# Two context-attention layers: score matmuls as 64 by 64 tiles, keys two batches ahead through a scratch in device memory

## The reference, cut to what matters

```python
# L3_xattn (L1_xattn: no _l2norm, no bq, scores times D**-0.5, a boolean mask instead of attn_bias)
q = (x @ Wq + bq).reshape(B, Lq, H, D).transpose(0, 2, 1, 3)     # B=8, Lq=64, H=16, D=16
k = (y @ Wk).reshape(B, Ly, H, D).transpose(0, 2, 1, 3)          # Ly=1601
v = (y @ Wv).reshape(B, Ly, H, D).transpose(0, 2, 1, 3)
q = _l2norm(q) * scale_mul
k = _l2norm(k)
attn = jnp.einsum('bhqd,bhkd->bhqk', q, k) + attn_bias
attn = jax.nn.softmax(attn, axis=-1)
oup = jnp.einsum('bhqk,bhkd->bhqd', attn, v)
return oup.transpose(0, 2, 1, 3).reshape(B, Lq, C) @ Wo + bo
```

## Time and profile before

| what | value |
|---|---|
| median of 3 runs | 2486.56 us (2485.36 to 2490.42) |
| the profiled execution | 2501.07 us, span 2499.3 us |
| PE busy in the span | 2236.3 us (89%) |
| PEld, DVE, ACT, POOL busy | 57%, 66%, 50%, 32% |
| batches 0 to 7 of the first layer, from the first L3417 of each | 386.05 to 726.26 us |
| the same of the normed layer | 1863.67 to 2258.00 us |

### The profile page before, as it was taken

One profiled execution on the slowest core, in us unless ns is written; L12 is line 12 of the kernel. 1 busy time (PEld: TensorE's weight loads), 2 busy tenths in 40 slices (PEclk: granted clock), 3 DMA queues, 4 the chain that ended last, 5 costly groups with the idle time before them and its releaser, 6 DMA issues. The chain is left out here.

```text
span 2499.3 us, 50978 instructions
## 1 busy us (share of the span) xinstructions
PE 2236.3 (89%) x20593; PEld 1417.7 (57%) x20650; DVE 1650.0 (66%) x3182; ACT 1243.2 (50%) x2071; POOL 808.3 (32%) x660
## 2 busy tenths in 40 slices
PE   6885779999978889999999999699879999998898
PEld 4764445666654555656655666356546555566554
DVE  4987456555548756888888854644576666665577
ACT  2326234555554225555555554566436555563565
POOL 5610052233206112321233300045445455433254
PEclk8998899999989989999999999899999999999999
DMA  3200453423313047676776764133322323220231
GB/s 113 71 7 1 144 136 103 107 78 106 79 66 106 13 118 144 121 133 133 151 146 122 125 113 80 34 102 102 116 67 67 86 69 86 69 67 23 71 96 60
DMA packets 358618, 226.84 MB, mean 91 GB/s; under 512 B 289913, under 2 KB 326610, under 8 KB 358386
## 3 DMA queue, kind: packets, MB, share of 16 engines
q1 hardware_dynamic: 355314, 215.20, 35.5%
q0 software_dynamic: 3072, 8.39, 1.2%
HBM read 114.87 MB, written 0.52 MB: 46 GB/s over the span
## 5 line engine op out<-in xcount | busy, mean ns | idle before, releaser
L3950 POOL TENSOR_TENSOR l2x_rows<-l2x_rows,l2x_one 128x256 f16<-128x256 f32 (+1 forms) x91 | 89.2, 1006 | 379.6 <-DVE l2x_rows L1507 354.5
L100 PE MATMUL PS<-hot 128*128 128x512 f16 x460 | 134.3, 427 | 82.1 <-DVE l0a_g L1119 17.5
L4054 PE MATMUL PS<-l2x_rows,l2x_pth 128*128 128x512 f16 x832 | 200.3, 379 | 1.7 <-DVE l2x_mean L4263 1.7
L3711 DVE CUSTOM_DVE_ANT_0 l1x_junk<-PS,l1x_bias 128x1024 bf16<-128x1024 f32 (+1 forms) x128 | 123.2, 991 | 73.6 <-PE PS L3371 72.7
L4256 DVE TENSOR_TENSOR l2x_pl<-l2x_sc,l2x_ph 128x1664 f16<-128x1664 f32 x64 | 125.1, 1954 | 44.6 <-ACT l2x_ph L4133 43.9
L4151 ACT ACTIVATE l2x_meanT<-PS 128x256 f32<-128x256 f32 x64 | 24.5, 383 | 250.5 <-PE PS L4016 250.5
L4241 DVE CUSTOM_DVE_ANT_0 l2x_sc<-PS,l2x_bias 128x1665 f32<-128x1665 f32 x64 | 120.9, 1889 | 36.3 <-issue 35.0
L3711 DVE CUSTOM_DVE_ANT_0 l3x_junk<-PS,l3x_bias 128x1024 bf16<-128x1024 f32 (+1 forms) x128 | 123.6, 991 | 24.3 <-PE PS L3371 21.6
L4008 PE MATMUL PS<-l2x_kh,l2x_qth 128*128 128x512 f16 (+1 forms) x512 | 131.9, 339 | 1.5 <-issue 1.5
L4008 PE MATMUL PS<-l2x_kh,l2x_qtl 128*128 128x512 f16 (+1 forms) x512 | 131.9, 339 | 0.0
L4008 PE MATMUL PS<-l2x_kl,l2x_qth 128*128 128x512 f16 (+1 forms) x512 | 131.9, 339 | 0.0
(11 more groups left out here) (866 smaller groups left out, 6109.0 us busy)
## 6 DMA issues: line engine op xcount, KB each, us to landing
l2f_unit<-in_L_ffn_units_dram SPq DMA_DIRECT2D x36, 384.0 KB, 3.1
l3f_unit<-in_L_ffn_units_dram SPq DMA_DIRECT2D x34, 384.0 KB, 3.0
l1x_kst<-l1x_kh SPq DMA_DIRECT2D x128, 100.1 KB, 2.2
l3x_kst<-l3x_kh SPq DMA_DIRECT2D x128, 100.1 KB, 2.2
l2x_rows<-in_ctx_dram SPq DMA_DIRECT2D x8, 1536.0 KB
l1x_ctx<-in_ctx_t_dram SPq DMA_DIRECT2D x7, 1601.0 KB, 7.3
l3x_ctx<-in_ctx_t_dram SPq DMA_DIRECT2D x7, 1601.0 KB, 7.0
l1x_kst<-l1x_kl SPq DMA_DIRECT2D x64, 100.1 KB, 2.2
```

The lines of the kernel that those rows point to most:

```text
L100: self.nc.tensor.matmul(self.PS[:, bank, :], self.hot[:, 0:P], self.hot[:], start=True, stop=True)
L3711: v.tensor_tensor_reduce(junk[:, slot(it), 0:n], slot_banks(it)[:, 0:n], bias[:, 0 if normed else b % 2, at:at + n], 1.0, LOWEST, ALU.add, ...
L3950: last = nc.gpsimd.tensor_tensor(high[:, at], of[:, at], one[0:p, at].unsqueeze(2).unsqueeze(3).to_broadcast([p, i, NC, P]), ALU.mult)
L4054: nc.tensor.matmul(PS[:, ACC, :], pth[:, u % 2, m, :], rows2[:, b % 2, :, :, m, :], start=(m == 0), stop=False)
```

## The change

Score matmuls work on one head each: 49 rows (high, low, the maximum's row at 32, high) against 64 columns, with the heads of a pair in rows 0 to 48 and 64 to 112 of `qst` and `kst`, and outputs in partitions 0 to 63 or 64 to 127. `A` becomes 4 pairs of pairs by 4 chunks of 401 keys, four matmuls and two VectorE reductions each. `turned` is one block for both halves, and its next call waits until both were read. Keys are made two batches ahead (K, N, I, U of batch b+2 in batch b, later in `steps`; batch 0 makes those of batches 1 and 2, by `opening_steps` and `second_keys`). `kh` and `kl` are written to a scratch `spill` in device memory and read back in six DMAs per chunk, with one semaphore per chunk. ACT and DVE do both halves' work of tile m first and then the items of both steps. The context is split in two parts of columns. In the normed layer the bias goes in as high and low part by two sets of matmuls. `ON_VECTOR` stays at tiles 0 to 3 in both layers.

```diff
-    A = [("A", u, h) for u in range(R) for h in range(NH)]
+    A = [("A", v, j) for v in range(QV) for j in range(NCH)]
     if normed:
-        steps = [[("K", 0, 0)], [("K", 0, 1)], [("N", 0, 0), R_], [("N", 0, 1), ("I", 0, 0)], [("U", 0, 0), ("I", 0, 1), ("V", 0, 0)],
-                 [E, ("U", 0, 1)], [("V", 1, 0)], [("K", 1, 0)], [("K", 1, 1)],
-                 [O_, ("N", 1, 0)], [("N", 1, 1), ("I", 1, 0)], [("U", 1, 0), ("I", 1, 1), ("V", 2, 0)],
-                 [P_, A[0], ("U", 1, 1)], [A[1], A[2]], [("V", 3, 0)], [A[3], A[4]], [A[5]], [A[6]], [A[7], A[8]],
-                 [A[9]], [("M", 0, 0), A[10]], [A[11]], [A[12]], [A[13], A[14]], [A[15]], [("M", 1, 0)]]
+        steps = [[V_[0]], [], [R_, V_[1]], [], [E], [V_[2]], [V_[3]], [O_], [A[0]], [A[1], A[2]], [A[3]], [A[4]], [P_, A[5]], [A[6], A[7]],
+                 [K_[0]], [K_[1], A[8]], [N_[0], M_[0]], [N_[1], I_[0], A[9]], [U_[0], I_[1], A[10]], [U_[1], K_[2], A[11]],
+                 [K_[3], A[12]], [N_[2], A[13]], [N_[3], I_[2], A[14], A[15]], [U_[2], I_[3]], [U_[3]], [M_[1]]]
+        second_keys = {18: [K_[0]], 19: [K_[1]], 20: [N_[0]], 21: [N_[1], I_[0]], 22: [U_[0], I_[1], K_[2]], 23: [U_[1], K_[3]],
+                       24: [N_[2]], 25: [N_[3], I_[2], U_[2], I_[3], U_[3]]}
...
     else:
-        steps = [[("K", 0, 0)], [], [("K", 0, 1), R_], [("K", 1, 0)], [E], [("K", 1, 1)], [("V", 0, 0)], [O_], [A[0]], [A[1]],
-                 [("V", 1, 0), A[2]], [A[3]], [P_, A[4]], [("V", 2, 0), A[5]], [A[6]], [A[7]], [("V", 3, 0), A[8]], [A[9]],
-                 [("M", 0, 0), A[10]], [A[11]], [A[12]], [A[13]], [A[14]], [A[15]], [], [("M", 1, 0)]]
+        steps = [[V_[0]], [], [R_], [V_[1]], [E], [V_[2]], [V_[3], A[0]], [O_, A[1]], [A[2], A[3]], [A[4]], [A[5]], [A[6]], [P_, A[7]],
+                 [A[8]], [K_[0]], [A[9], M_[0]], [A[10]], [K_[1]], [A[11]], [A[12]], [K_[2]], [A[13]], [A[14]], [A[15], K_[3]], [],
+                 [M_[1]]]
+        second_keys = {20: [K_[0]], 22: [K_[1]], 23: [K_[2]], 25: [K_[3]]}
...
                 def stack(b, c):
+                    sp.wait_ge(spilled[c], (b + 1) * SPILL)
                     if b >= 2:
                         sp.wait_ge(turned_made, (b - 1) * STEPS)
-                    for j in range(RC):
-                        for g, part in enumerate((kh, kl, kh)):
-                            sp.dma_start(kst[g * F:(g + 1) * F, b % 2, c * RC + j, :],
-                                         part[j * F:(j + 1) * F, c, :]).then_inc(stacked[c * RC + j], 16)
+                    for at, x in ((0, 0), (DH, 1), (ROW + 1, 0)):
+                        for r in range(2):
+                            sp.dma_start(kst[r * S + at:r * S + at + DH, b % 2, c * RC:(c + 1) * RC, :],
+                                         spill[x, c].rearrange("(j r d) n -> r d j n", r=2, d=DH)[r]).then_inc(stacked[c], 16)
...
-                        for i, at, n in pieces(*halves[j]):
-                            last = nc.tensor.matmul(PS[:, bank + i, 0:n], qst[0:3 * F, b, c, :, :],
-                                                    kst[0:3 * F, b % 2, c, at:at + n], start=True, stop=True)
+                        at, n = chunks[j]
+                        for i in range(2):
+                            for r in range(2):
+                                rows = slice(r * S, r * S + KROWS)
+                                last = nc.tensor.matmul(PS[i * S:(i + 1) * S, bank + r, 0:n], qst[rows, b, 2 * c + i, :],
+                                                        kst[rows, b % 2, 2 * c + i, at:at + n], start=True, stop=True)
...
+                    for u in range(R):
+                        for at, w_ in keys:
+                            for r in range(2):
+                                rows = slice(r * S, r * S + KROWS)
+                                last = nc.tensor.matmul(PS[at:at + w_, S_BANK + r, u * S:(u + 1) * S],
+                                                        kst[rows, b % 2, u, m * P + at:m * P + at + w_], qst[rows, b, u, :],
+                                                        start=not on_tensor, stop=not on_tensor or u == R - 1, skip_group_check=True)
...
-                            pe.wait_ge(exp_done, e - G2 + 1)
+                            pe.wait_ge(exp_done, e)
...
-                            for it in step_before(b, m * G2 + g):
+                            exp(b, m, g)
+                        for g in range(G2):
+                            for it in at_step(b, m * G2 + g):
                                 item(it)
-                            exp(b, m, g)
```

More of the change, by code:

```diff
@@ L3420, in turned @@
-                    last.then_inc(turned_made, 1)
+                        for x in range(2 if normed else 1):
+                            for at, w_ in keys:
+                                for r in range(2):
+                                    half = slice(r * S, (r + 1) * S)
+                                    of_bias = fsp[half, x, :] if normed else bias[half, b % 2, :]
+                                    nc.tensor.matmul(PS[at:at + w_, S_BANK + r, :], of_bias[:, m * P + at:m * P + at + w_], one_hot[half, :],
+                                                     start=(x == 0), stop=False, skip_group_check=True)
```

264 lines of the change are left out of this document (154 added, 110 removed).

## The result

The changed kernel takes 2805.82 us (2799.44 to 2813.48, four runs) against 2488.49 us of the kernel before on the same chip: ratio 1.1276, 95% interval 1.1242 to 1.131. It is slower by 317 us, where I forecast some 30. Both loops got slower. Windows cut at the first matmul of `turned` (now L3479) of a batch, in the same order as the earlier trace rows: first batch, two middle ones, the last but one and the last; the first layer, then the normed one. Columns: stretch, its length, busy us (instructions) of PE, PEld, DVE, ACT and POOL, granted clock, DMA share, GB/s.

A forecast was written before the change was run, and what follows sets the result against it. PE was taken to bound both loops, with slots and DVE taking over after the change. First layer +0.3 and normed layer +29.7 made +30: 2501.1 to 2531 us profiled, 2516 on the median; range 2463 to 2566.

The forecast's parts named there:

- In the loop they have over a batch's slack: Scratch write and six reads a chunk, some 5 and 8 us, hidden in the loop except the normed layer's first half chunk.
- PE's standing lets the clock fall: Listed as proving the forecast wrong: standing PE drops the clock to its lower level, 1.2 GHz; no size given.
- `turned`: 8 x 56 = 0.45 us a key tile becomes 8 x 32 = 0.26, times 13: PE's `turned` matmuls: sets of four run together at 32 ns instead of 56, saving 2.5 us a batch.
- rival 2: Slower still: only two 64 by 64 tiles run together on PE; 2566, up to 2616 us; chance 0.12.
- the row of `values`: Earlier trace of `values`: four heads in different columns, all rows, 56 ns for four; evidence against only two running together.
- PE's work, less 5.8 and 3.6 us: PE's work a batch falls by 5.8 us in the first layer and 3.6 in the normed one.
- Standing of 10.4 us: PE's summed waits in a first-layer middle batch, behind A, K(0), tiles 9 and 11, the end and small ones.
- rival 1: Faster: PE's standing is half of that walked, excess under 4 us a batch; 2471 us; chance 0.24.
- my walk: Item-by-item schedule of a middle batch: PE work 36.6 plus standing 10.4 us in first layer, 44.5 plus 12.2 in normed.
- Middle batches of 45.7 to 47 and 55.4 to 56.7: Middle-batch lengths, without and with O and P: first layer as before, normed layer 2.3 us longer.
- Batch 0 at 55.5 and 76: First batch of each layer makes two batches' keys: 55.5 us against 42.8, and 76 against 51.7.
- Rival 3: It comes out even: saving 30 us larger than summed, most easily in the normed layer's batch 0; 2487 us; chance 0.11.

The follow-up runs named there:

- e2: Changed kernel, scratch reads from batch 2 on go to 64 partitions of one key unit instead of 16 of four, same bytes, keys misplaced; 2711.01 us, 1.083.
- e3: Changed kernel, scratch laid out so each partition's four units form one contiguous 12.8 KB row, still read into 16 partitions; 2817.85 us, 1.126.
- e4: Kernel before, plus bursts of eight 15- or 16-partition reads in seven first-layer batches, into spare partitions, data unused; 2529.91 against 2504.22 us, 1.0113.
- e15: e2 plus warming matmuls where PE stands: 30 and 37 a middle batch, 5 more ahead of O and 5 ahead of the first key tile; 2693.85 us, 1.0742.
- e18: e15 with the thirteenth key tile's `turned` loop turned round, all 64-key matmuls before the one-key ones; keys misplaced; 2647.81 us, 1.0628.
- e17: e12 with the thirteenth key tile's `turned` loop turned round, all 64-key matmuls before the one-key ones; 2674.71 us, 1.0749.
- e12: Changed kernel's 64 by 64 tiles with the order of the kernel before, no scratch, stacked keys copied on chip by 48 copies a batch; 2707.13 us, 1.0883.
- e14: Kernel before, old tiles, without the products of the weights' low parts in K and V, both layers; 2451.05 against 2503.96 us, 0.9776.

## Why the prediction was wrong

The direction was right and the size was not. On the profiled run I had 2531 us, and it took 2807. The batches account for it: over my figures, the walked batches 1 to 5 lie 87 and 95 us, the first ones 16 and 33, batch 6 16 and 20, batch 7 3 and 2; together 272 of 276. The starts of the loops nearly cancel: the first layer's came 9.6 us sooner (forecast 5), and the stretch between it and the normed layer's grew by 16.7 (forecast 5).

- *"In the loop they have over a batch's slack"* and *"I cost that at nothing; if the cover is gone it is 1 to 3 us a batch."* This is the step that failed most. I took each read by its landing, alone, and asked only who waits for the data. Twelve reads into 16 partitions hold all DMA engines for 19 us at 125 GB/s, and the victim is PE, which needs instructions: 9 to 12 us a walked batch, 111 us in all (changed kernel against e2). e3 excludes the rows, e4 shows that no reader of the data is needed, and the fetches on q8 show what PE waited for. It is 111 of some 290 us; e2, without it, would still have been far outside my range.
- *PE's standing lets the clock fall.* I named it as what would make me wrong and gave it neither price nor chance, since in the earlier trace rows no batch shows it. It fell behind stands of 1.0 to 2.2 us, among others, though a stand of 1.6 us in the kernel before did not bring it down; I can't say what decides. e15 gives back 22 us net of its own fillers; what the fall costs in full was not isolated. From the clock in e2 (0.84 to 0.91 in the five batches, mean 0.864, over 55 us: 15 us at the lower level, in which half as much work is done) I estimate 7.5 us a batch there, and 2.8 in the normed layer (0.956 over 63).
- *"`turned`: 8 x 56 = 0.45 us a key tile becomes 8 x 32 = 0.26, times 13."* Right for twelve tiles: 32 matmuls in one block of 0.43 us, of which a single one is 0.19. So four tiles run together, rival 2 is out, and the row of `values` was the better guide. For the thirteenth tile it was wrong by 1.8 us: I counted 43 changes of shape a batch and overlooked 15 within that block. 30 us.
- *PE's work, less 5.8 and 3.6 us.* It is less 4.0 and 1.7 (e18). A is as summed (7.0 to 4.7 us, -2.4). `turned` and the mask in the first layer were to save 4.5 and save 2.3 (9.6 to 7.3). The thirteenth tile, which I priced like the others in both, has 0.7 of the difference even with its loop turned round; the changes of shape behind these blocks, which I had summed apart, are in the 7.3 as well. The rest was not taken apart.
- *Standing of 10.4 us.* e2 shows the stands where I had walked them: 2.19 ahead of M(0) (2.4), 1.49 and 0.86 behind the first A (2.8 in tiles 3 to 5), 1.03, 0.64 and 0.63 in tile 11 to 12 (2.9). With the small ones they sum to 8.3 a batch, and 11.2 in the normed layer (12.2). That is 5.1 and 7.3 more than the kernel before has, where I had 7.0 and 8.2 and rival 1 needed under 4, so rival 1 is out by its own condition; the first layer lies about midway between my walk and the rival.
- *Middle batches of 45.7 to 47 and 55.4 to 56.7.* With the three costs repaired 49.8 and 62.6 remain, 3.6 and 6.7 over the walk. In the first layer PE's own work has 3.1 of it, 38.9 instead of 35.8 in the mean, and the fillers with what standing is left take 10.8 where I had walked 10.4 of standing. In the normed layer the clock is still 0.97 and PE's work is 4 to 5 us above the walk.
- *Batch 0 at 55.5 and 76.* 71.7 and 108.6, and no repair changed it (72.3 and 106.4 in e18). In the normed layer PE stands 13.6 us for A0: its reads were issued at 2035.6, when POOL had split the second set of keys, and landed at 2049.07. I had POOL's line in the walk, but not the reads' 13 us behind it. The rest is a clock of 0.79 and A packed two to a step. This was not taken apart.
- *Batch 6 at 34.8 and 36.8* was 50.7 and 56.6, with reads and a low clock as in the others; 41.2 and 46.9 repaired. *Batch 7 at 24.3 and 26.3* was 27.2 and 28.7, and 24.8 and 26.0 once the thirteenth tile was repaired.
- *DVE's 1.4 us more for A* was no cost: DVE's busy time of a middle batch rose by 0.4 to 1.2 us in the first layer and not at all in the normed one.

Rival 3 (even) needed all of this to be cheap. Had the steps above been priced, 111 + 30 + 52 for the clock (5 x 7.5 + 5 x 2.8) would have made some 2709, of 2806 measured. What is left, about 97 us, is in size what the first batches (16 + 33) and the middle batches of e18 (5 x 3.6 + 5 x 6.7) lie over the walk; the first batches stay unexplained for the most part.

No version with the new tiles beats the kernel before; the best ones that compute the reference are e17 (2674.71) and e12, and both still stand for their late copies. e14, which leaves a third of K's and V's products out, is the only one below it.
